# Second attention: keys and values copied as one by ACT, and another order of the steps in a slot

## What is computed

```python
xn = _layernorm(x)                     # x: (1, 1024, 512) f32
x = x + attn0(xn) * silu(ffn0(xn))     # 8 heads of 8; a router, low-rank experts
xn = _layernorm(x)
q = (xn @ Wq.T) -> 32 heads of 128; k, v = (xn @ Wk.T), (xn @ Wv.T) -> 8 heads of 128
q, k = rmsnorm(q) * q_norm_w, rmsnorm(k) * k_norm_w
attn = softmax(q k^T / sqrt(128) + alibi, causal)          # 4 query heads share k and v
s = (attn v) @ Wo.T
w_up, w_down = NF4[codes] * absmax     # both of 512 x 1376, blocks of 64
x = x + s * silu(relu(xn @ w_up + ... ) @ w_down + ...)    # both with low-rank parts
```

## Time and profile before

| | us |
|---|---|
| three timed runs | 1464.19, 1468.36, 1468.0; median 1468.0 |
| the profiled execution | 1465.94 |
| its span on the core | 1464.0 |
| PE / DVE / ACT / POOL busy | 1373.5 / 981.1 / 855.6 / 634.2 |

### The profile page before, as it was taken

The page is one execution under the profiler, slowest core; times in us unless marked ns, Lnnn a source line. Parts: engine busy times, 40 slices in busy tenths (PEclk is TensorE's granted clock), DMA queues, the critical chain, the costliest instruction groups (busy, mean ns, idle before and its releaser), DMA issues.

```text
span 1464.0 us, 21333 instructions
## 1 busy us (share of the span) xinstructions
PE 1373.5 (94%) x7350; PEld 1076.4 (74%) x7350; DVE 981.1 (67%) x1834; ACT 855.6 (58%) x2103; POOL 634.2 (43%) x973
## 2 busy tenths in 40 slices
PE   4989988899999999999999999999999999989997
PEld 3733336688888788877888887888778877768786
DVE  6665655577777776777777777777687777675333
ACT  2345564566667666676666666676666666563211
POOL 4322365544355544444444554544444545433311
PEclk9998998899999999999999999999999999999999
DMA  4200031101020110012011101101020111114010
GB/s 141 65 1 1 1 97 58 44 1 59 4 71 21 39 53 22 30 30 74 1 60 35 40 24 36 60 15 40 21 73 4 42 35 38 37 58 135 15 58 29
DMA packets 35882, 61.01 MB, mean 42 GB/s; under 512 B 9056, under 2 KB 13280, under 8 KB 35776
## 3 DMA queue, kind: packets, MB, share of 16 engines
q1 hardware_dynamic: 35776, 59.66, 12.9%
HBM read 49.68 MB, written 9.96 MB: 41 GB/s over the span
## 4 chain that ended last, share of the span: by engine, by line
PE 75%; DVE 12%; issue 7%; ACT 3%; POOL 2%; DMA 1%; POOLq 0%; DVEq 0%; SPq 0%; ACTq 0%
PE T L2298 7%; PE T L1910 7%; PE T L1912 6%; PE T L1911 6%; PE S L1912 5%; PE S L1911 5%; PE S L1910 5%; PE WB L1910 4%; PE VB L1912 4%; PE VB L1910 4%; PE WB L1911 4%; PE WB L1912 4%; PE VB L1911 4%; PE VB L2066 2%; PE T L2181 2%
## 5 line engine op out<-in xcount | busy, mean ns | idle before, releaser
L881 POOL TENSOR_TENSOR RI<-SM,C 128x1 f32<-128x1 f32 x256 | 142.9, 558 | 506.8 <-ACT PB L1214 505.7
L1682 DVE CUSTOM_DVE_ANT_0 PB<-S,REL,SLC 128x128 f32<-128x128 f32 (+7 forms) x256 | 204.5, 813 | 80.3 <-PE S L1912 78.7
L1214 ACT ACTIVATE PB<-PB,NM 128x128 f32<-128x128 f32 (+7 forms) x256 | 198.9, 777 | 69.2 <-DVE NM L1682 64.3
L1287 ACT ACTIVATE R<-T 128x512 fp32r<-128x512 f32 x288 | 170.5, 593 | 100.6 <-PE T L2298 98.6
L1689 DVE TENSOR_TENSOR R<-T,R 128x512 fp32r<-128x512 f32 x288 | 197.5, 689 | 42.1 <-ACT R L1287 23.7
L882 POOL TENSOR_SCALAR PB<-PB,RI 128x128 f32<-128x128 f32 (+7 forms) x256 | 214.5, 838 | 25.2
L2298 PE MATMUL T<-C,PB 128*128 128x128 f32 x1152 | 176.6, 276 | 11.9 <-DVE R L1689 6.7
L2298 PEld LDWEIGHTS T<-C,PB 128*128 128x128 f32 x1152 | 134.2, 140 | 48.0 <-DVE R L1689 18.0
L1194 ACT ACTIVATE JUNK<-WB 128x128 bf16<-128x128 f32 x252 | 66.2, 277 | 93.1 <-PE WB L1912 93.1
L1910 PE MATMUL T<-R 128*128 128x512 f32 x256 | 104.0, 406 | 3.9 <-issue 2.1
L1912 PE MATMUL T<-R 128*128 128x512 f32 x256 | 100.5, 393 | 0.0
(11 more groups left out here) (299 smaller groups left out, 3521.1 us busy)
## 6 DMA issues: line engine op xcount, KB each, us to landing
RAW<-w SPq DMA_DIRECT2D x86, 256.0 KB, 2.8
DQ<-codes SPq DMA_DIRECT2D x16, 352.0 KB, 3.5
DQ<-absmax SPq DMA_DIRECT2D x16, 352.0 KB, 2.9
dequantised<-DQ SPq DMA_DIRECT2D x16, 352.0 KB, 2.2
PB<-x SPq DMA_DIRECT2D x12, 256.0 KB, 3.3
PB<-dequantised SPq DMA_DIRECT2D x5, 512.0 KB, 4.5
PB<-x_scratch SPq DMA_DIRECT2D x8, 256.0 KB, 3.9
out<-PB SPq DMA_DIRECT2D x8, 256.0 KB, 2.0
```

The costliest lines, as they stand in the source:

```text
L881: ch.link(e.tensor_tensor(RI[:, k:k + 1], SM[:, k:k + 1], C[:, C_EXP + 5:C_EXP + 6], ALU.pow))
L1214: e.activation(pb(m, a, 0, L), pb(m, a, 0, L), ACT.Exp, scale=-1.0, bias=NM[:, k:k + 1], accum_out=SM[:, k:k + 1]).then_inc(exp_done, 1)
L1287: e.activation(r(PT + AT[i, ("PV", kb)] % 3 * 1024, 512), T[AT[known, it] % 2][:, :], ACT.Copy).then_inc(t_act, 1)
L1682: e.tensor_tensor_reduce(out=pb(m, a, 0, L), in0=bank[:, 0:L], in1=REL[:, TOK - L:TOK], scale=SLC[:, a:a + 1], scalar=3.0e38, op0=ALU.add, ...
```

## The change

`copy_kv` has ACT copy k and v (256 columns) from the T bank to `KVS` at once; DVE copies no k and only passes `t_free` on. A new item `KS` has ACT square k from `KVS`, and at `QN` ACT scales k (`scale_k`, with a semaphore `k_ready` of its own); DVE scales q alone, and the transposes of q wait for q alone. The items of a slot come in another order: T0 ahead of the second exponential in even slots; W chunks 2 and 3 behind T2 and T3; Q chunks 0 and 1 at the start of j = 5, released by TensorE after each quarter of PQ (`q_used`), Q chunks 2 and 3 ahead of the last exponential. DVE's dequantisation steps leave `DA` and `DB` for `DD`, directly behind PKV, and `DC`, behind E; the last two (selection, absmax) pass to the next two slots. ACT's lines stay at `DA` and `DB`. SP loads codes and absmax and stores the chunk in the second slot of four. Not shown: the renaming of `VS` to `KVS` in other places, the semaphores.

```diff
@@ -215,20 +215,23 @@
     put("V", when=0 < n <= STEPS - NT)
     weights("K", 0, 1)
     weights("W", 0, 1)
+    weights("Q", 0, 1)
     put("PQ", when=s2)
     head(0, "S")
     head(1, "S")
     head(0, "EX")
     put("PKV", when=kv)
+    put("DD")
     head(0, "NR")
     if j % 2 == 0:
+        head(2, "S")
+        keys(0)
+        put("KS", when=kv)
         put("IV", when=s2)
-        head(2, "S")
         head(1, "EX", "NR")
-        keys(0)
         head(3, "S")
+        keys(1)
         head(2, "EX", "NR")
-        keys(1)
         put("QN", when=s2)
         ffn(STEPS - 2, ("FU", 0))
         put("WO", when=n > 0)
@@ -238,35 +241,32 @@
         ffn(STEPS - 4, ("FA", 2), ("FA", 3), ("FZ", 1))
         keys(*range(2, nk))
     else:
-        weights("W", 2)
         keys(0)
+        put("KS", when=kv)
         put("IV", when=s2)
         head(2, "S")
-        head(1, "EX")
         keys(1)
         ffn(STEPS - 1, ("FU", 1))
-        head(1, "NR")
-        weights("W", 3)
+        head(1, "EX", "NR")
         head(3, "S")
-        head(2, "EX")
         keys(2)
         ffn(STEPS - 1, ("FV", 1))
-        weights("Q", 0, 1)
-        head(2, "NR")
+        weights("W", 2)
+        head(2, "EX", "NR")
+        keys(3)
+        weights("W", 3)
+        weights("Q", 2, 3)
         head(3, "EX", "NR")
-        keys(3)
         put("QN", when=s2)
         put("WO")
         put("DA")
         ffn(STEPS - 5, ("FA", 0), ("FA", 1))
         ffn(STEPS - 3, "FB")
-        keys(4)
-        weights("Q", 2, 3)
-        keys(5, 6, 7)
+        keys(4, 5, 6, 7)
     put("QK", when=s2)
     ffn(STEPS - 2, ("FH", 0))
     ffn(STEPS - 1, ("FH", 1), "UP")
-    put("E", "DB")
+    put("E", "DC", "DB")
     ffn(STEPS - 2, ("FL", 0))
...
@@ -746,25 +748,27 @@
                     sp.wait_ge(fw_split, j - 3)
                 sp.dma_start(STAGE[j % 4], wd_dram[:, j * 1024:(j + 1) * 1024]).then_inc(in_fw[j % 4], 16)
 
-            def load_codes(g, i):
-
-                if isinstance(g, int):
-                    cc = (LOOP * g + i) // 4
-                    if cc:
-                        sp.wait_ge(dq_selected, cc)
-                    else:
-                        sp.wait_ge(w_free, W_AT["WO", NT - 1] + 1)
-                    sp.dma_start(CODES, codes[cc * P:(cc + 1) * P, :]).then_inc(in_codes, 16)
+            def load_codes(chunk):
+
+                if chunk:
+                    sp.wait_ge(dq_selected, chunk)
                 else:
-                    sp.wait_ge(dq_selected, g * 4 + i // 4)
-                    sp.dma_start(CODES, codes[bass.ds(g * (4 * P) + i // 4 * P, P), :]).then_inc(in_codes, 16)
+                    sp.wait_ge(w_free, W_AT["WO", NT - 1] + 1)
+                sp.dma_start(CODES, codes[chunk * P:(chunk + 1) * P, :]).then_inc(in_codes, 16)
+
+            def load_absmax(chunk):
+
+                sp.wait_ge(dq_selected, chunk + 1)
+                sp.dma_start(DQ[:, 3, :], absmax[chunk * P:(chunk + 1) * P, :]).then_inc(in_absmax, 16)
 
             def slot(g, i):
                 jj = i % 4
                 j = i % NT
                 known = LOOP * g + i if isinstance(g, int) else i
-                if jj == 0:
-                    load_codes(g, i)
+                if i == 0:
+                    load_codes(0)
+                if jj == 1 and i > 1:
+                    load_absmax(i // 4 - 1)
                 if known == 0 and isinstance(g, int):
                     w1_first("K", 1, 0)
                     w1_first("K", 1, 1)
...
+                if jj == 1 and i > 1:
+
+                    load_codes(i // 4)
+                    sp.wait_ge(dq_scaled, i // 4 + 1)
+                    sp.dma_start(wd_dram[:, bass.ds((i // 4 - 1) * DQN, DQN)], DQ[:, 1, :]).then_inc(out_dq, 16)
...
@@ -807,14 +816,8 @@
                     sp.wait_ge(t_full, AT[STEPS - 2, "last"] + 1)
                     load_tile(2)
                     load_tile(3)
-                if jj == 0 and not (isinstance(g, int) and known == 0):
-
-                    sp.wait_ge(dq_scaled, g * 4 + (i // 4 + 1))
-                    sp.dma_start(wd_dram[:, bass.ds(g * (4 * DQN) + (i // 4 - 1) * DQN, DQN)], DQ[:, 1, :])\
-                        .then_inc(out_dq, 16)
-                if jj == 3:
-                    sp.wait_ge(dq_selected, g * 4 + i // 4 + 1)
-                    sp.dma_start(DQ[:, 3, :], absmax[bass.ds(g * (4 * P) + i // 4 * P, P), :]).then_inc(in_absmax, 16)
+                if i == STEPS - 1:
+                    load_absmax(i // 4)
 
             slots(sp, slot)
...
 
-            def squares_k(m, tcount, tk):
+            def copy_kv(m, tcount, tk):
                 act.wait_ge(t_full, tcount)
-                e.activation(JUNK[:, m % 2 * 5 + 4, :], tk[:, 0:HD], ACT.Square, accum_out=SQ[:, m % 2, 4:5]).then_inc(squares, 1)
-                e.activation(VS[:, (m - 2) % 4, :], tk[:, HD:2 * HD], ACT.Copy).then_inc(t_act, 1)
+                e.activation(KVS[:, (m - 2) % 4, :], tk[:, 0:2 * HD], ACT.Copy).then_inc(t_act, 1)
+
+            def squares_k(m, tcount):
+                act.wait_ge(t_act, tcount)
+                e.activation(JUNK[:, m % 2 * 5 + 4, :], KVS[:, (m - 2) % 4, 0:HD], ACT.Square, accum_out=SQ[:, m % 2, 4:5])\
+                    .then_inc(squares, 1)
+
+            def scale_k(m, icount, tprev):
+
+                act.wait_ge(inv_ready, icount)
+                act.wait_ge(t_full, tprev)
+                e.activation(QN[:, 4 * HD:5 * HD], KVS[:, (m - 2) % 4, 0:HD], ACT.Copy, scale=INV[:, m % 2, 4:5])\
+                    .then_inc(k_ready, 1)
 
             def high_q(m, tq, bq):
                 act.wait_ge(t_full, tq)
@@ -1297,7 +1311,12 @@
                     elif it == "PKV":
                         if known == 0:
                             act.wait_ge(out_x1[3], 16)
-                        squares_k(i + 2, at(g, i, "PKV") + 1, T[AT[known, "PKV"] % 2])
+                        copy_kv(i + 2, at(g, i, "PKV") + 1, T[AT[known, "PKV"] % 2])
+                    elif it == "KS":
+                        squares_k(i + 2, at(g, i, "PKV") + 1)
+                    elif it == "QN":
+                        if known + NT < STEPS:
+                            scale_k(i + 2, n0 + 3, at(g, i - 1, "KT") + 1 if known else T_BASE)
...
                         kind, c = it[1], it[2]
-                        if c == 0 and kind == "Q":
-
-                            act.wait_ge(t_full, at(g, i, "PKV") + 1)
+                        if c < 2 and kind == "Q":
+
+                            act.wait_ge(q_used, i // NT * 2 + c + 1)
                         elif c == 0 and kind == "K":
 
...
 
-            def copy_k(tcount, tk, tprev):
-                dve.wait_ge(t_act, tcount)
-
-                dve.wait_ge(t_full, tprev)
-                e.tensor_copy(QN[:, 4 * HD:5 * HD], tk[:, 0:HD]).then_inc(t_free, 1)
...
                 q = e.tensor_tensor(QN[:, 0:4 * HD].rearrange("p (a n) -> p a n", a=4),
                                     bank[:, :].rearrange("p (a n) -> p a n", a=4),
                                     INV[:, k, 0:4].unsqueeze(2).to_broadcast([P, 4, HD]), ALU.mult)
                 q.then_inc(free, 1)
-                if tcopy is not None:
-                    dve.wait_ge(t_free, tcopy)
-                    e.tensor_scalar(QN[:, 4 * HD:5 * HD], QN[:, 4 * HD:5 * HD], INV[:, k, 4:5], None, ALU.mult)\
-                        .then_inc(qk_ready, 1)
 
             def low_q(m, tq, bq):
...
 
-            def combine(g, i, part):
-
-                jj = i % 4
-                chunk = g * 4 + i // 4
-                if jj == 0 and part == 0 and not (isinstance(g, int) and LOOP * g + i == 0):
+            def combine(i, part):
+
+                jj, chunk = i % 4, i // 4
+                if (jj, part) == (1, 1) and chunk:
                     dve.wait_ge(in_absmax, chunk * 16)
                     e.tensor_tensor(DQ[:, 1, :], DQ[:, 1, :], DQ[:, 3, :], ALU.mult).then_inc(dq_scaled, 1)
-                todo = {(1, 0): (1,), (1, 1): (2,), (2, 0): (3,), (2, 1): (5,), (3, 0): (6,), (3, 1): (7,)}
-                for ln in todo.get((jj, part), ()):
-                    dve.wait_ge(line, chunk * 8 + ln + 1)
-                    b, op = (1, ALU.min) if ln < 4 else (2, ALU.max)
-                    if ln not in (1, 5):
-                        dve.wait_ge(line_used, chunk * 6 + {2: 1, 3: 2, 6: 4, 7: 5}[ln])
-                    e.tensor_tensor(DQ[:, b, :], DQ[:, b, :], DQ[:, 3, :], op).then_inc(line_used, 1)
-                if (jj, part) == (3, 1):
-
+                ln = {(1, 0): 1, (2, 1): 2, (2, 0): 3, (3, 1): 5, (3, 0): 6}.get((jj, part))
+                if ln:
+                    use_line(chunk, ln)
+                if (jj, part) == (0, 1) and chunk:
+                    use_line(chunk - 1, 7)
                     ch.link(e.tensor_scalar(CODES, CODES, 8, None, ALU.bitwise_and))
-                    hold(dve, line_used, chunk * 6 + 6, v_passed)
```

(55 more changed lines are left out.)

18 lines of the change are left out of this document (10 added, 8 removed).

## The result

The changed kernel takes 1480.1 us (median of 5 runs, 1476.4 to 1482.0); beside it the kernel before took 1468.4 (median of 5, 1464.2 to 1469.7). The ratio is 1.0086, 95% interval 1.0070 to 1.0103: slower by 0.9%. The forecast was 1481. The profiled execution has a span of 1478.3 us and took 1480.1; the one before had 1464.0 and 1465.9, so the two traces differ by 14.3 us.

The account below looks back on a forecast made before the run. TensorE, busy 94% of the span, was taken as the bound, so only its stalls could change. Seven rounds at +1.9 us (+13.3) and +1 at the end, +14.3 on 1465.9, gave 1480, stated as 1481; 8-in-10 range 1463 to 1491.

Parts of the forecast that it names:

- The chain over DD: From PKV through DD and T0's low half to the output projection: +0.95 us in j = 2, +1.33 in j = 4.
- The copy's price: ACT's copy of K and V, 256 columns: 0.38 us, bounds 0.27 and 0.59.
- What the order gives: Stalls freed without DD's cost, mostly in j = 1, 5 and 6: about 3.8 us a round.
- What the change removes: DVE loses K's copy (0.29 us) and scaling (0.28, or 0.99 held up by POOL); ACT's added work costs nothing.
- j = 0 to 7 of the change itself: Net terms by slot of a round: 0, -0.3, +0.95, +0.15, +1.33, -0.3, -0.2, +0.27; sum +1.9 us.
- The eighth round: Last round, without K and V, where DVE meets POOL less: 0.
- The end: Last combining steps, masking and selection in one piece on DVE before the feed-forward's first tiles: about +1 us.
- SP's queue: Loads of absmax and codes and the store move to the second slot of four, behind chunk loads: costs nothing.
- A: Rival: DVE's combining step starts before POOL's division in j = 2 and 4; +0.4 us a round, 1470; chance 0.2.
- C: Rival: the new gap in j = 4 lowers TensorE's clock, up to 1.7 us more each; 1493; chance 0.07.
- B: Rival: faster; as A, with ACT's copy at 0.27 us and j = 1 keeping 0.9; 1458; chance 0.15.
- D: Rival: gains of j = 1, 5, 6 come whole and cover j = 2 and 4; 1466 to 1468; chance 0.08.

Follow-up runs that it names:

- e5: The kernel of e1 with DA (ACT's lines and DVE's combining step) of even slots behind the slot's last transposed block: 1448.6 us.
- e1: The changed kernel with the dequantisation steps and SP's transfers back in their old places (DA and DB, no DC or DD): 1456.9 us.
- e4: The changed kernel with DD one place later, behind head 2's bias pass and T0's low half: 1478.5 us.
- e3: The changed kernel with POOL's inverse norms ahead of its division of head 0 instead of behind it: 1467.2 us.
- e6: The kernel of e1 with POOL's inverse norms ahead of its division of head 0, the same edit as e3: 1456.7 us.
- e7: The kernel before with K and V copied as one by ACT, K's squares and scaling on ACT, items in the old order: 1476.0 us.
- e9: The kernel of e1 with K copied and scaled by DVE as before, so the new order of items alone: 1454.6 us.
- e14: The changed kernel with DVE's steps of the last dequantisation piece back at DA and DB from slot 61 on: 1476.3 us.
- e2: The kernel before with only the new places of the dequantisation steps (DC and DD) and of SP's loads and store: 1554.6 us.
- e10: The kernel of e9 with DA of even slots behind the slot's last transposed block: 1452.2 us.
- e8: The kernel of e2 with SP's code load and store ahead of the Q chunk loads in its queue: 1511.0 us.
- e12: The kernel before with DA of even slots behind the slot's last transposed block, and nothing else: 1462.4 us.

## Why the prediction came true, and where it didn't

**What bounds the kernel.** Held. DVE's load does not matter: it has 15 us less to do and the kernel is slower, e5 keeps e1's work and is 8 us faster.

**The chain over DD.** Held, in place, size and cause: +0.94 in j = 2 (+0.95 forecast), +1.24 in j = 4 (+1.33). The link from POOL's end to the step's end measured 0.73, with 0.74 forecast. In slot 12 the step started 0.6 us behind the end of ACT's copy, where I had said 0.25, and so lasted 1.10 and not the 1.4 that I had named as a sign; it didn't matter, since POOL's end decided (in slot 20 it is 0.25 and 1.46). e4, which moves DD alone, takes away the whole 1.24 of j = 4. e1 takes away only 0.70, since the old step at DA holds 0.54 of its own there (e5). e3 and e6 show that the collision is worth 0.75 of the one term and, in most rounds, 0.56 of the other.

**The copy's price.** Held: 0.38 for 256 columns.

**What the order gives.** The round's sum is right only because two errors cancel. I put 3.8 us a round on what would be gained without DD; e1 shows 1.3. I put the gain of j = 1 to 1.5 and it is 0.94; of j = 5 to 0.7 and it is 0.70; of j = 6 to 0.4 and it is 0.12; "j = 0, 3, 7 some 0.4 each" is -0.10, 0.20 and -0.02; and j = 4, which I didn't count, loses 0.54. So for DD I had implied 5.7 (3.8 and 1.9) and it costs 3.0. One step that failed is the first part of "What the change removes": DVE's copy of K was counted as time ahead of the T blocks' low halves. It lay beside ACT's high half (e7), and the sentence that ACT's added work "costs nothing unless it lands ahead of a T copy" had the answer in it; it does land there. K and V by ACT thus lose 0.3 us a round (e1 against e9): 0.47 in j = 4, less 0.26 gained in j = 6. The rest of the missing 2.5 us, some 0.5 in j = 1, 0.3 in j = 6 and over 1 in j = 0, 3 and 7, was put on the order, and e9, the order alone, doesn't show it either; behind the terms of j = 0, 3 and 7 stood no row.

**j = 0 to 7 of the change itself.** All within 0.2 of the forecast: the terms I had netted (-0.3, -0.2, +0.27, +0.15) measured -0.40, -0.23, +0.11, +0.06, and j = 1 -0.14 for -0.3. That the netted terms fit is luck, since both the gains and DD's cost in them were put too high. In j = 1 the forecast had the parts right: the selection met POOL's division, and absmax landed when DVE arrived (at 6.37 us into slot 9, and the scaling started at 6.39). Seven rounds: +10.6 for +13.3; in e14's trace they are +8.7.

**The eighth round.** Forecast 0; slots 56 to 60 are 1.0 us shorter than before. Mis-sized by about that.

**The end.** Forecast +1; it is +5.2. I saw the steps bunch, but not that step 3, ACT's line and step 5 alternate on one buffer, nor that the clock would fall behind the gap. This term is the largest miss. Its 4.2 us too little stand against 2.7 too much for the seven rounds and 1.0 for the eighth: that the total came out right to 1 us is partly luck.

**SP's queue.** "Nothing" was right for this change, and for the reason given, the chunk loads being released early. e2 shows that it is right only because the order is changed too: with the old order the same queue costs 6.25 us a round.

**Rivals.** A (the step slips in before POOL) did not happen in j = 2 and 4: POOL was first by 0.13 and 0.54 us. It did in j = 0. C (the clock falls behind j = 4's gap): 1.39 us of idle left the clock at 1.00. It fell at the end instead, behind 3.54. B asked for a copy of 0.27 us and 0.9 kept in j = 1, and D for the order's gains in full beside DD; the copy took 0.38 and j = 1 kept 0.14. B's figure was also reckoned wrongly: its -1.7 a round counts from the kernel before, so that it stood for 1456, not 1458.

**Left open.** Why the clock fell in e1 and e10 behind a gap of 2.37 us that left it at 1.00 in e5 and e9, and why the gains put on j = 0, 3, 6 and 7 are not there.

## What to carry to other kernels

A step that is moved to even out an engine's load has to be priced at its new place by the chain that passes there: ahead of each instruction that frees a bank, ask how long until the bank's next user, and whether POOL is busy in SBUF just then. Before a copy is counted as saved, look at what its successor waits for; here it waited for another engine. Parts of a change can need one another (the chunk order and SP's queue), so a part that costs nothing within the change may cost 44 us alone (e2 less e8).

## What the runs showed of the hardware

- A DVE instruction that met a running POOL instruction ended 0.73 to 0.76 us behind it, with a length of 0.89 of its own: behind divisions (slots 10 and 12) and behind POOL's split of a weight chunk (e5, e10, e12).
- Back-to-back DVE instructions keep POOL out for longer than one of them: a division that met a combining step of 0.89 us and a masking of 0.52 took 2.03 instead of 1.12 (slot 8).
- A selection over 704 columns took 1.00 us alone (at 1340.14) and 1.86 behind a division of 1024 columns. The winner can hang on hundredths: with 0.09 us between their starts (after) the division kept the selection out, with 0.05 to 0.08 it was itself kept out, though it had started first (1.92 to 1.95 us instead of 1.12, e14).
- TensorE's clock stayed at 1.00 behind gaps of 1.39 and 1.62 us; behind 3.12 (e10) it was 0.50 for 3.9 us, and 0.61 for the 3 us behind 3.54; behind e2's gap of 4.47 us slot 13 has a mean of 0.94. The gap alone does not tell: behind one of 2.37 to 2.38 us in the same place of slot 61 it fell in e1 and e10 (0.53 and 0.54 over the next 3 us) and stayed at 1.00 in e5 and e9, and in the changed kernel it was 0.57 behind two gaps of 0.45 and 1.00.
- The time ahead of slot 0, which no edit touches, differs between the profiles by up to 8 us (slot 0 starts 3.7 us earlier than before in e9 and 4.4 later in e12), with a granted clock of 0.97 and 0.93 over the first 250 us, 0.95 in the kernel before. Much of the spread of a kernel's runs may come from there; comparing slots within the traces leaves it out.
